# A row normalised in two halves, and its bias moved from VectorE to GpSimd, in a lattice attention kernel

## The chip, the cores and the metric

The kernel runs on one core of one Trainium2 chip. The metric is the device time in microseconds of one execution; the median of three runs is given. Engines: PE is TensorE, DVE VectorE, ACT ScalarE, POOL GpSimd, SP SyncE. Each takes its instructions in the order of the program and waits on semaphores for the others.

## The reference, cut to what matters

Eight sequences of 1024 tokens, 64 channels wide. An embedding comes first, then one "lattice" attention layer (8 heads of 64, so 8 x 8 = 64 pairs of sequence and head, called heads below), then a block of causal attention and a mixture of experts. The change is in the lattice layer:

```python
scores = einsum('bhqd,bhkd->bhqk', q, k) / sqrt(64)
int_scores = (abs(scores) * 1618).astype(int32)          # ttt_filter
chaos = int_scores % 9 in (0, 3, 6)
scores = scores * where(chaos, 1 / PHI, 1.0)
attn = softmax(scores, axis=-1)
attn = attn * (sin(C1 * attn) * exp(-attn**2 / PHI) + cos(C2 * attn))
ctx = einsum('bhqk,bhkd->bhqd', attn, v)
```

The softmax subtracts each row's maximum. The kernel gives it to the exponential as a bias, one number a row: bias = -EXPSCALE * maximum.

## The kernel before, in words

A head's scores are 1024 x 1024 fp32. They stand in `att` as eight tiles of 128 partitions (queries) by 1024 columns (keys); such a tile is called a row (of tiles) below, rows 0 to 7 of a head. `att` has two buffers, one for even, one for odd heads.

In `lattice`, the work on a head is cut into instructions that are placed on a time axis of steps by lists written out by hand. `SCORE` has the steps of the 16 score pieces (128 x 512, two to a row), `EXP` those of the 8 rows' exponentials, `GAUSS` and `SINE` those of the 8 transposed tiles on the way through exp(-x^2/PHI), sin and cos, `AV` those of the products with the values. A head stretches over three times `STEPS` = 88 steps; each pass `iteration(t, par)` walks through the 88 steps and issues what the lists put there for the heads t, t - 1 and t - 2. Every engine has a walk of its own through the same lists, and so a fixed order of its instructions; offsets such as `FILT` = 9 or `NORM` = 2 say how many steps behind the list's entry an instruction stands. A step is a place in that order, not a time: semaphores alone hold an engine up.

The instructions by name, with their lines:

- Score piece n of a head: PE product into one of three PSUM banks (L650); ACT absolute value (L502); POOL near op, to the nearest integer (L429, `RND` 2); DVE keep op (L561, `KEEP` 5); POOL factor op (L423, `FACT` 6); DVE filter op, which multiplies, writes `att` and keeps the row's maximum in `mx` (L570, `FILT` 9).
- Bias of row u: DVE, one column, `nb` = -EXPSCALE * `mx` (L578, `BIAS` 23 steps behind the row's second score piece).
- Row j: ACT exponential in place, with the row's sum (L466); DVE reciprocal of the sum (L537, `NORM` 2); POOL normalisation in place, times the reciprocal and times TURN (L418, `NORM` 2), 128 x 1024; DVE turn rounding of the row into `nturn`, bf16 (L549, `TURNS` 8), which waits for that row's normalisation.
- PE transposes (L608, `fill`), eight blocks of 128 x 128 for a pair of key blocks of four rows: tiles 0 to 3 wait until rows 0 to 3 are normalised, tiles 4 to 7 until all eight are. Each tile is transposed twice, once for the Gaussian part (ACT L495, L507, DVE L543, the ag product) and once for cosine and sine (ACT L478, DVE L520, PE L624, ACT L484, DVE L555).
- PE products with the values (L667), copied out by DVE (L526, L528); for each second head PE's fold (L674) and DVE's add to `hres` (L532).

The order on POOL by steps, around the change: near ops at 2, 5, 9, factor ops at 6, 9, 13, then the rows of the head before at 14, 16, 17, 19, 20, near ops at 23, 25, row 5 at 26, a factor op at 27, row 6 at 28, a factor op at 29, a near op at 30, row 7 at 34, and from there on factor and near ops alone. `held` is a wait with an empty instruction behind it on the sequencer. The semaphore `weights` counts the normalised rows, `filtered` DVE's filter ops, `bias` the biases.

Of the kernel before, what the change touches and what calls it, by code (L numbers as in the profile page):

```python
# [6 lines left out]
ALU = mybir.AluOpType  # L7
# [9 lines left out]
TB = S // P  # L17
# [8 lines left out]
EXPSCALE = 3.0 / (1618.0 * PHI * PHI)  # L26
TURN = C1 / (2.0 * math.pi)
# [3 lines left out]
def wait(eng, s, v):  # L31

    if not isinstance(v, int) or v > 0:
        eng.wait_ge(s, v)


def held(eng, s, v):

    if not isinstance(v, int) or v > 0:
        eng.wait_ge(s, v)  # L40
        eng.nop(nofuse=True)
# [226 lines left out]
def lattice(nc, ident, hres, xT_dram, wvo, Wq, bq, Wk, bk):  # L268

    RING = 4  # L270
    with ExitStack() as ctx:
# [15 lines left out]
        att = sb("att", [P, 2, TB, S])  # L287
# [5 lines left out]
        nb = sb("nb", [P, 2, TB])  # L293
# [102 lines left out]
        @block.gpsimd  # L396
        def _(pool):
            nc.gpsimd.memset(x[D:D + 1, :], 1.0).then_inc(consts, 1)
            pool.wait_ge(consts, 1)
            nc.gpsimd.memset(negI[:], 0.0).then_inc(consts, 1)  # L400
            pool.wait_ge(consts, 2)
            nc.gpsimd.affine_select(out=negI[:], in_=negI[:], compare_op=ALU.not_equal, fill=-1.0,
                                    base=0, pattern=[[-1, P]], channel_multiplier=1).then_inc(consts, 1)
            nc.gpsimd.memset(halfpi[:], math.pi / 2).then_inc(consts, 1)
            pool.wait_ge(consts, 4)
            nc.gpsimd.tensor_tensor(stack[:], ident[:, 0:D], ident[:, D:P], ALU.add).then_inc(consts, 1)
            pool.wait_ge(consts, 5)
            nc.gpsimd.memset(qT[:], 0.0).then_inc(consts, 1)
            pool.wait_ge(consts, 6)
            nc.gpsimd.memset(kT[:], 0.0).then_inc(consts, 1)  # L410

            def iteration(t, par):
                for s in range(STEPS):
                    for g, p, a in stages(t, par, s):
                        if a - NORM in EXP:
                            j = EXP.index(a - NORM)
                            held(pool, recip, TB * g + j + 1)
                            nc.gpsimd.tensor_scalar(att[:, p, j], att[:, p, j], rs[:, j:j + 1], TURN,  # L418
                                                    ALU.mult, ALU.mult).then_inc(weights, 1)
                        if a - FACT in SCORE:  # L420
                            n = SCORE.index(a - FACT)
                            held(pool, kept, NTILE * g + n + 1)
                            nc.gpsimd.tensor_scalar(mag[:, n % 4], mag[:, n % 4], 1.0, PHI,  # L423
                                                    ALU.mult, ALU.add).then_inc(factor, 1)
                        if a - RND in SCORE:
                            n = SCORE.index(a - RND)
                            held(pool, mags, NTILE * g + n + 1)
                            held(pool, kept, NTILE * g + n - 3)
                            nc.gpsimd.tensor_scalar(near[:, n % 4], mag[:, n % 4], 1.0 / 6.0, 1.0,  # L429
                                                    ALU.add, ALU.mult).then_inc(rounded, 1)  # L430

            over_heads(pool, iteration)
# [80 lines left out]
        def _(dve):  # L513
            def iteration(t, par):
                for s in range(STEPS):
# [22 lines left out]
                    for g, p, a in stages(t, par, s):  # L538
                        if a - AG in GAUSS:
                            d = GAUSS.index(a - AG)  # L540
                            wait(dve, gauss, TB * g + d + 1)
                            wait(dve, tmul, TB * (g - 1) + d + 1)
                            nc.vector.tensor_tensor(pair(ag[:, d]), turn_pair(d), pair(work[:, d % RING]),  # L543
                                                    ALU.mult).then_inc(agd, 1)
                        if a - TURNS in EXP:
                            j = EXP.index(a - TURNS)
                            wait(dve, nned, TB * g)
                            wait(dve, weights, TB * g + j + 1)
                            nc.vector.tensor_scalar(nturn[:, j], att[:, p, j], ROUND, -ROUND,  # L549
                                                    ALU.add, ALU.add).then_inc(turned, 1)  # L550
                        if a - P3 in SINE:
                            k = SINE.index(a - P3)
                            wait(dve, sined, TB * g + k + 1)
                            wait(dve, agd, TB * (g + 1))
                            nc.vector.tensor_tensor(sinb[:, k % RING], sinb[:, k % RING], ag[:, k],  # L555
                                                    ALU.mult).then_inc(tmul, 1)
                    for g, p, a in stages(t, par, s):
                        if a - KEEP in SCORE:
                            n = SCORE.index(a - KEEP)
                            wait(dve, rounded, NTILE * g + n + 1)  # L560
                            nc.vector.scalar_tensor_tensor(mag[:, n % 4], near[:, n % 4], 1.0, mag[:, n % 4],  # L561
                                                           ALU.mult, ALU.is_gt).then_inc(kept, 1)
                        if a - FILT in SCORE:
                            n = SCORE.index(a - FILT)
                            u, cols = n // 2, slice(n % 2 * 512, (n % 2 + 1) * 512)
                            wait(dve, factor, NTILE * g + n + 1)
                            wait(dve, filtered, NTILE * g + n)
                            wait(dve, xpose, NX * (g - 1))
                            dve.nop(nofuse=True)
                            nc.vector.tensor_tensor_reduce(  # L570
                                att[:, p, u, cols], mag[:, n % 4], score_bank(n), 1.0,
                                mx[:, p, n - 1:n] if n % 2 else -3.0e38, ALU.mult, ALU.max,
                                mx[:, p, n:n + 1]).then_inc(filtered, 1)
                        if a - BIAS in SCORE and SCORE.index(a - BIAS) % 2 == 1:
                            n = SCORE.index(a - BIAS)
                            u = n // 2
                            wait(dve, filtered, NTILE * g + n + 1)
                            nc.vector.tensor_scalar(nb[:, p, u:u + 1], mx[:, p, n:n + 1], -EXPSCALE, None,  # L578
                                                    ALU.mult).then_inc(bias, 1)

            over_heads(dve, iteration)

# [1 line left out]
        def _(pe):  # L584
# [16 lines left out]
            def fill(g, p, k):  # L601

                half = k // HALF
                wait(pe, weights, TB * g + TB // 2 * (half + 1))
                for c in range(2):
                    kt = 2 * k % TB + c
                    for i in range(4):
# [986 lines left out]
```

## Time and profile before

| | us |
|---|---|
| median of 3 runs | 5767.98 (5761.31 to 5770.59) |
| the profiled execution, its own time | 5762.87 |
| its span | 5761.0 |
| PE busy | 4760.1 (83%) |
| DVE busy | 4565.5 (79%) |
| ACT busy | 3985.3 (69%) |
| POOL busy | 2866.8 (50%) |
| lines of POOL in the lattice: factor op L423, near op L429, row L418 | 880.3, 779.2, 734.3 |
| bias of DVE, L578, x404 between 700 and 4200 us | 58.2 |

The span runs from the first to the last instruction. Busy times are sums over an engine's instructions; where they overlap waits of others they say nothing of what bounds the kernel. The first of the 64 heads' rows is normalised at 169 us, the last at 4554 us, and the lattice has the same pattern in between: heads about 69 us apart.

### The profile page before, as it was taken

The page shows a single profiled execution, that of the slowest core. Times are in us where ns is not written, and L with a number is a line of the kernel's source. Part 1 is how long each engine was busy: PE and PEld are TensorE (multiplying, and loading weights), DVE is VectorE, ACT ScalarE, POOL GpSimd, SP SyncE. Part 2 cuts the span into 40 slices and gives each one's busy share as a digit, 9 for nine tenths or more (in the row PEclk, how much of TensorE's full clock was granted, in tenths as well). Part 3 has the DMA queues.
Part 4 walks back from the last instruction along what each step waited for, and adds up shares of the span by engine and source line. Part 5 has one row for each costly group of instructions (what it writes and reads, how often), then busy time and mean ns, then how long its engine had stood idle before and what let it go on. Part 6 is the DMA issues. An engine that isn't in the chain of part 4 may idle for free. (4 is left out here: it accounts for less than half of the span.)

```text
span 5761.0 us, 97974 instructions
## 1 busy us (share of the span) xinstructions
PE 4760.1 (83%) x27689; PEld 2815.3 (49%) x27689; DVE 4565.5 (79%) x8035; ACT 3985.3 (69%) x5494; POOL 2866.8 (50%) x3215
## 2 busy tenths in 40 slices
PE   4788888888888888888888888888888769996999
PEld 2444444444444444444444444444444445554666
DVE  4788888888888888888888888888888656666664
ACT  2777787777877777787778778777777634443332
POOL 5555555555555555555555555555555334443233
PEclk9899999999999999999999999999999879998999
DMA  1000000000000000000000000000000000000000
GB/s 22 11 8 8 8 8 8 8 8 8 8 8 9 8 10 8 8 8 8 8 8 8 8 8 8 8 9 10 8 8 8 3 9 1 2 2 15 3 5 8
DMA packets 34197, 45.35 MB, mean 8 GB/s; under 512 B 24521, under 2 KB 24585, under 8 KB 34058
## 3 DMA queue, kind: packets, MB, share of 16 engines
q1 hardware_dynamic: 32010, 43.49, 2.8%
q0 software_dynamic: 2048, 0.14, 0.1%
q8 instruction: 72, 1.18, 0.1%
q14 instruction: 67, 0.55, 0.0%
HBM read 39.40 MB, written 4.19 MB: 8 GB/s over the span
## 5 line engine op out<-in xcount | busy, mean ns | idle before, releaser
L608 PE MATMUL banks<-ident,att 128*128 128x128 f32 x8192 | 1220.4, 300 | 533.4 <-DVE ag L543 339.2
L608 PEld LDWEIGHTS banks<-ident,att 128*128 128x128 f32 x8192 | 1027.9, 155 | 1094.0 <-DVE ag L543 539.6
L429 POOL TENSOR_SCALAR near<-mag 128x512 int32<-128x512 f32 x1024 | 779.2, 761 | 1257.0 <-ACT mag L502 1135.3
L650 PE MATMUL banks<-kT,qT 128*128 128x512 f32 x2048 | 1131.4, 642 | 60.3 <-DVE mx L570 59.0
L423 POOL TENSOR_SCALAR mag<-mag 128x512 f32<-128x512 f32 x1024 | 880.3, 864 | 567.9 <-DVE mag L561 532.5
L667 PE MATMUL outp<-work,vo 128*64 128x512 f32 x2048 | 960.6, 602 | 0.0
L667 PE MATMUL outp<-sinb,vo 128*64 128x512 f32 x2048 | 960.6, 602 | 0.0
L561 DVE SCALAR_TENSOR_TENSOR mag<-near,mag 128x512 f32<-128x512 int32 x1024 | 798.1, 784 | 110.1 <-POOL near L429 109.9
L478 ACT ACTIVATE work<-banks,halfpi 128x1024 f32<-128x1024 f32 x512 | 570.5, 1115 | 413.6 <-PE banks L608 311.5
L418 POOL TENSOR_SCALAR att<-att,rs 128x1024 f32<-128x1024 f32 x512 | 734.3, 1434 | 226.6 <-DVE rs L537 184.7
L520 DVE TENSOR_TENSOR work<-banks,work 128x1024 f32<-128x1024 f32 x512 | 624.7, 1220 | 158.2 <-ACT work L478 153.5
L495 ACT ACTIVATE work<-banks 128x1024 f32<-128x1024 f32 x512 | 521.1, 1021 | 301.1 <-PE banks L608 297.7
L555 DVE TENSOR_TENSOR sinb<-sinb,ag 128x1024 f32<-128x1024 f32 x512 | 673.7, 1316 | 2.1 <-ACT sinb L484 2.1
L543 DVE TENSOR_TENSOR ag<-banks,work 128x1024 f32<-128x1024 f32 x512 | 612.7, 1217 | 68.4 <-ACT work L507 62.2
L502 ACT ACTIVATE mag<-banks 128x512 f32<-128x512 f32 x1024 | 603.6, 590 | 47.0 <-PE banks L650 45.3
L484 ACT ACTIVATE sinb<-banks 128x1024 f32<-128x1024 f32 x512 | 523.7, 1023 | 115.6 <-PE banks L624 110.1
L466 ACT ACTIVATE att<-att,nb 128x1024 f32<-128x1024 f32 x512 | 582.2, 1138 | 0.8
L549 DVE TENSOR_SCALAR nturn<-att 128x1024 bf16<-128x1024 f32 x512 | 421.3, 833 | 145.8 <-POOL att L418 145.8
L507 ACT ACTIVATE work<-work 128x1024 f32<-128x1024 f32 x512 | 526.7, 1054 | 8.1
L667 PEld LDWEIGHTS outp<-work,vo 128*64 128x64 f32 x2048 | 248.9, 136 | 495.8 <-issue 481.1
L624 PEld LDWEIGHTS banks<-negI,nturn 128*128 128x128 bf16 x4096 | 260.9, 103 | 439.0 <-DVE work L520 357.1
L624 PE MATMUL banks<-negI,nturn 128*128 128x128 bf16 x4096 | 332.8, 227 | 134.5 <-DVE work L520 134.5
(197 smaller groups left out, 6387.9 us busy)
## 6 DMA issues: line engine op xcount, KB each, us to landing
x<-xT_dram SPq DMA_DIRECT2D x128, 256.0 KB, 3.5
xT_dram<-xT SPq DMA_DIRECT2D x8, 256.0 KB, 3.0
out<-hres SPq DMA_DIRECT2D x8, 256.0 KB, 2.6
base<-in_L_tok_turns,idx POOLq DMA_INDIRECT x64, 2.4
wqk<-in_L_attn_Wq SPq DMA_DIRECT2D x64, 16.0 KB
wqk<-in_L_attn_Wk SPq DMA_DIRECT2D x64, 16.0 KB
wqk<-in_L_attn_bq SPq DMA_DIRECT2D x64, 0.2 KB
wqk<-in_L_attn_bk SPq DMA_DIRECT2D x64, 0.2 KB
```

Of the source, the lines that this page charges most:

```text
L418: nc.gpsimd.tensor_scalar(att[:, p, j], att[:, p, j], rs[:, j:j + 1], TURN, ALU.mult, ALU.mult).then_inc(weights, 1)
L423: nc.gpsimd.tensor_scalar(mag[:, n % 4], mag[:, n % 4], 1.0, PHI, ALU.mult, ALU.add).then_inc(factor, 1)
L429: nc.gpsimd.tensor_scalar(near[:, n % 4], mag[:, n % 4], 1.0 / 6.0, 1.0, ALU.add, ALU.mult).then_inc(rounded, 1)
L502: nc.scalar.activation(mag[:, n % 4], score_bank(n), ACT.Abs).then_inc(mags, 1)
L520: nc.vector.tensor_tensor(pair(work[:, k % RING]), turn_pair(k), pair(work[:, k % RING]), ALU.mult).then_inc(acd, 1)
L543: nc.vector.tensor_tensor(pair(ag[:, d]), turn_pair(d), pair(work[:, d % RING]), ALU.mult).then_inc(agd, 1)
L555: nc.vector.tensor_tensor(sinb[:, k % RING], sinb[:, k % RING], ag[:, k], ALU.mult).then_inc(tmul, 1)
L561: nc.vector.scalar_tensor_tensor(mag[:, n % 4], near[:, n % 4], 1.0, mag[:, n % 4], ALU.mult, ALU.is_gt).then_inc(kept, 1)
L608: mm = nc.tensor.matmul(turn_pair(k)[:, c, i * P:(i + 1) * P], att[:, p, 4 * half + i, kt * P:(kt + 1) * P], ident[:], is_transpose=True, ...
L624: mm = nc.tensor.matmul(turn_pair(k)[:, c, i * P:(i + 1) * P], nturn[:, 4 * half + i, kt * P:(kt + 1) * P], negI[:], start=False, stop=Tru ...
L650: nc.tensor.matmul(score_bank(n), qT[:, p, (n // 2) * P:(n // 2 + 1) * P], kT[:, p, (n % 2) * 512:(n % 2 + 1) * 512], start=True, stop=Tru ...
L667: mm = nc.tensor.matmul(outp[rows], vo[:, kt, :], term[:, k % RING, c * 512:(c + 1) * 512], start=(kt == 0), stop=(kt == TB - 1), skip_gro ...
```

## The change

It does two things on the same steps. Each normalisation becomes two instructions of 512 columns, each of which adds one to `weights`; the waits for `weights` count twice as far, so that all who waited for a whole row, or four, still do. The bias is computed by POOL instead of DVE, at the same step (23 behind the row's second score piece); on POOL it is issued within a step ahead of the factor and near ops of the same head, and it waits for DVE's filter op through `held`. On DVE, bias and wait go. The instruction gets a second operation, + 0.0.

```diff
                             j = EXP.index(a - NORM)
                             held(pool, recip, TB * g + j + 1)
-                            nc.gpsimd.tensor_scalar(att[:, p, j], att[:, p, j], rs[:, j:j + 1], TURN,
-                                                    ALU.mult, ALU.mult).then_inc(weights, 1)
+                            for c in range(2):
+                                cols = slice(c * 512, (c + 1) * 512)
+                                nc.gpsimd.tensor_scalar(att[:, p, j, cols], att[:, p, j, cols], rs[:, j:j + 1], TURN,
+                                                        ALU.mult, ALU.mult).then_inc(weights, 1)
+                        if a - BIAS in SCORE and SCORE.index(a - BIAS) % 2 == 1:
+                            n = SCORE.index(a - BIAS)
+                            u = n // 2
+                            held(pool, filtered, NTILE * g + n + 1)
+                            nc.gpsimd.tensor_scalar(nb[:, p, u:u + 1], mx[:, p, n:n + 1], -EXPSCALE, 0.0,
+                                                    ALU.mult, ALU.add).then_inc(bias, 1)
                         if a - FACT in SCORE:
...
                             wait(dve, nned, TB * g)
-                            wait(dve, weights, TB * g + j + 1)
+                            wait(dve, weights, 2 * (TB * g + j + 1))
...
-                        if a - BIAS in SCORE and SCORE.index(a - BIAS) % 2 == 1:
-                            n = SCORE.index(a - BIAS)
-                            u = n // 2
-                            wait(dve, filtered, NTILE * g + n + 1)
-                            nc.vector.tensor_scalar(nb[:, p, u:u + 1], mx[:, p, n:n + 1], -EXPSCALE, None,
-                                                    ALU.mult).then_inc(bias, 1)
...
-                wait(pe, weights, TB * g + TB // 2 * (half + 1))
+                wait(pe, weights, 2 * TB * g + TB * (half + 1))
```

## Rows read from the trace of the kernel before

**Rows 1.** Busy time in one stretch, with the granted clock (PEclk, 1.00 is 2.4 GHz).
```profile
700.00:4200.00 3500.00, 2909.30 (x15956) 1656.81 (x15952) 3007.08 (x4970) 2769.24 (x3583) 1891.22 (x2015) 0.94 0.03 8
```

**Rows 2.** Groups, 700:4200: busy us, mean ns of one | idle before, who ended it.
```profile
L561 DVE SCALAR_TENSOR_TENSOR mag<-near,mag 128x512 f32<-128x512 int32 x806 | 628.9, 785 | 61.2 <-POOL near L429 61.2
L429 POOL TENSOR_SCALAR near<-mag 128x512 int32<-128x512 f32 x806 | 616.1, 764 | 992.6 <-ACT mag L502 895.6 <-DVE mag L561 71.5
...
L466 ACT ACTIVATE att<-att,nb 128x1024 f32<-128x1024 f32 x407 | 462.8, 1138 | 0.6
...
L549 DVE TENSOR_SCALAR nturn<-att 128x1024 bf16<-128x1024 f32 x402 | 330.0, 831 | 117.6 <-POOL att L418 117.6
```

**Rows 3.** Waits, 1000:4000: who, for whom: us in total, times, longest.
```profile
PE banks L608 <- POOL att L418: 132.6, 44, 3.0
```

**Rows 4.** Timeline of POOL, one head: start, us, what, count, idle before.
```profile
2113.20 0.62 POOL L429 TENSOR_SCALAR near<-mag 128x512 int32<-128x512 f32 x1
2114.70 0.62 POOL L423 TENSOR_SCALAR mag<-mag 128x512 f32<-128x512 f32 x1 [0.88 <-DVE mag L561]
2115.46 7.81 POOL L418 TENSOR_SCALAR att<-att,rs 128x1024 f32<-128x1024 f32 x5
...
2132.12 1.40 POOL L418 TENSOR_SCALAR att<-att,rs 128x1024 f32<-128x1024 f32 x1 [1.99 <-DVE rs L537]
```

**Rows 5.** Timeline of POOL, rows 0 to 3 of that head one by one.
```profile
2115.46 1.12 POOL L418 TENSOR_SCALAR att<-att,rs 128x1024 f32<-128x1024 f32 x1
2116.67 1.12 POOL L418 TENSOR_SCALAR att<-att,rs 128x1024 f32<-128x1024 f32 x1
2117.88 1.95 POOL L418 TENSOR_SCALAR att<-att,rs 128x1024 f32<-128x1024 f32 x1
2119.92 1.62 POOL L418 TENSOR_SCALAR att<-att,rs 128x1024 f32<-128x1024 f32 x1
```

**Rows 6.** Timeline of DVE, the same head.
```profile
2117.41 0.92 DVE L549 TENSOR_SCALAR nturn<-att 128x1024 bf16<-128x1024 f32 x1
...
2119.94 0.71 DVE L549 TENSOR_SCALAR nturn<-att 128x1024 bf16<-128x1024 f32 x1 [1.01 <-POOL att L418]
...
2125.44 0.14 DVE L578 TENSOR_SCALAR nb<-mx 128x1 f32<-128x1 f32 x1
2125.52 0.69 DVE L532 TENSOR_TENSOR hres<-outp,hres 128x512 f32 x1
```

**Rows 7.** Timeline of PE, the head before and this head.
```profile
2052.83 3.37 PE L608 MATMUL banks<-ident,att 128*128 128x128 f32 x16 [3.01 <-POOL att L418]
...
2121.60 1.97 PE L608 MATMUL banks<-ident,att 128*128 128x128 f32 x16 [3.01 <-POOL att L418]
```

**Rows 8.** POOL in the causal stage, 4600:5700: groups by width, then its timeline.
```profile
L862 POOL TENSOR_SCALAR c_pr<-c_pr,c_rs 128x1024 f32<-128x1024 f32 x32 | 35.8, 1119 | 50.8 <-DVE c_rs L1009 50.8
...
L862 POOL TENSOR_SCALAR c_pr<-c_pr,c_rs 128x512 f32<-128x512 f32 x32 | 22.1, 691 | 53.2 <-DVE c_rs L1009 53.2
...
L862 POOL TENSOR_SCALAR c_pr<-c_pr,c_rs 128x128 f32<-128x128 f32 x32 | 11.9, 372 | 38.7 <-DVE c_rs L1009 38.7
...
4718.22 0.91 POOL L862 TENSOR_SCALAR c_pr<-c_pr,c_rs 128x768 f32<-128x768 f32 x1 [2.74 <-DVE c_rs L1009]
4719.10 1.12 POOL L851 TENSOR_SCALAR c_qh<-c_q,c_own 128x1024 f32<-128x1024 f32 x1
```

**Rows 9.** Busy time around the two transposes of rows 7, with the granted clock.
```profile
2051.50:2056.00 4.50, 3.17 (x16) 3.17 (x17) 3.15 (x6) 1.27 (x3) 4.24 (x4) 0.62 0.00 0
2118.00:2124.00 6.00, 2.99 (x26) 2.40 (x23) 3.65 (x7) 3.79 (x7) 5.70 (x4) 1.00 0.00 0
```

**Rows 10.** Durations, ns min/median/max: near and keep ops, 700:4200; roundings, 1000:4000.
```profile
L429 POOL TENSOR_SCALAR near<-mag x806: 617/617/1556, 701.2 to 4193.7; 128x512 int32<-128x512 f32 x162
L561 DVE SCALAR_TENSOR_TENSOR mag<-near,mag x806: 670/687/1468, 703.6 to 4194.3; 128x512 f32<-128x512 int32 x162
...
L549 DVE TENSOR_SCALAR nturn<-att x349: 666/707/1148, 1004.3 to 3996.9; 128x1024 bf16<-128x1024 f32 x175
```

## The prediction

> **What bounds the kernel now.** I read the busy shares of a long steady stretch first, then who waits for whom, then the timeline of one head. No engine is full: DVE is busy 3007 of 3500 us (86%), PE 83%, ACT 79%, POOL 54% [rows 1]. So the order of the work across the four engines bounds it, and POOL, idle for nearly half of the time, can still be what the others wait for. It is: between 1000 and 4000 us PE waits for POOL's normalised rows 44 times, once a head (so a head takes some 69 us), 132.6 us together, 3.0 us a head [rows 3]. The timeline of one head says where. At 2115.46 POOL starts on the eight rows of a head; the first five run back to back, 7.81 us [rows 4]. Row 3, the fourth, ends at 2119.92 + 1.62 = 2121.54, and PE's transposes start at 2121.60, after 3.01 us with nothing to do [rows 5, 7]. I followed the waits back over 50 heads of the trace, from each instruction to the dependence, or the instruction before it on its engine, that ended last: this chain goes through rows 0 to 3 in every head, through row 4 in 21 of the 50, through one of rows 5 to 7 once: 4.4 rows a head. It comes to them along POOL: the factor op in front (2114.70, 0.62) ends 0.14 before row 0 starts [rows 4].
>
> One more thing is in these rows. An undisturbed row takes 1.12; row 2 takes 1.95 and row 3 1.62 [rows 5], since DVE's turn rounding (fp32 in, bf16 out) starts at the same moment and POOL stands still meanwhile. And the other way round: the rounding that starts at 2117.41, inside row 1, takes 0.92, the next 0.71 [rows 6]. A row and a rounding exclude each other.
>
> **The change, part by part.**
> (a) Each row in two halves. Another stage runs the same kind of POOL instruction, with a per-partition scalar, in eight widths: 1.119 at 1024 columns, 0.691 at 512, 0.372 at 128 [rows 8]. That is 0.83 ns a column and 0.26 us fixed. An undisturbed row of the lattice is 1.12 too, so a half is 0.691. The gap between two rows is 0.09 (2115.46 + 1.12 = 2116.58, the next starts at 2116.67) [rows 5]. So a row costs 2 x 0.691 + 0.09 - 1.12 = 0.35 us more. A rounding of DVE in between doesn't change that sum: it still waits for both halves, starts beside the first half of the next row, and holds that up as it now holds up the row. Nobody uses a half alone: the rounding of row j waits for 2(j + 1) halves, the transposes for all four rows of theirs. On the chain: 4.4 x 0.35 = 1.55 us a head. Rows 5 to 7 grow too, but they run between waits of POOL (row 7 at 2132.12 after 1.99 of idle time [rows 4]) and are on the chain in one head of 50: taken as nothing; were all eight rows on it, 8 x 0.35 = 2.8. The gap could be smaller: in another stage an instruction starts 0.03 before the one in front has ended (4718.22 + 0.91, then 4719.10) [rows 8], which makes 0.23 a row. I take 0.09, since it is the gap between these very instructions.
>
> (b) The bias leaves DVE. It shows 0.14 us, but the next instruction starts 0.08 after it (2125.44, 2125.52) [rows 6], so 0.07 to 0.08 of DVE's time; eight a head make 0.6. The chain as followed holds 1.6 of the eight: 1.6 x 0.07 = 0.11 us a head gained. Bounds: 0 and 0.6.
>
> (c) The bias comes to POOL, eight a head. No row shows a one-column tensor_scalar there. From below I take the fixed part of the near op, whose scalars are constants (0.617 at its fastest for 512 columns [rows 10], less 512 x 0.83 ns: 0.19), from above the 128-column instruction, 0.37 [rows 8]; value 0.2, with the gap 0.3. In POOL's order they stand at the steps 26, 44, 51, 60, 68, 74, 83 and 98, which is 10 of the next head. The one at 10 is the delicate one: it lies in front of the factor op of 2114.70, hence of all eight rows. But there POOL is idle for 0.88, waiting for DVE [rows 4]; without that cover it would be 0.3 a head. The one at 26 comes behind row 5, where the chain has left POOL; the other six stand where POOL waits for ACT or DVE (992.6 us of idle time before 806 near ops [rows 2]). Taken as nothing; bounds 0 and 8 x 0.3 = 2.4 a head. The new wait, for DVE's filter op, has always ended by then: ahead of each bias in POOL's order stands a factor op or a row whose own wait needs an instruction that DVE issues after that filter op. So nothing queues behind it. ACT's exponentials never waited for the bias (0.6 us idle before 407 of them [rows 2]) and the bias is ready many steps ahead of them on POOL as well.
>
> (d) TensorE's clock. PE's idle stretch before the transposes grows from 3.0 to 4.4 us. One head earlier the granted clock around this place is 0.62, here 1.00 [rows 9], and the same 16 transposes take 3.37 there and 1.97 here [rows 7]. A fall from 2.4 to 1.2 GHz so costs up to 1.4 us in a head. I take nothing, since the low level is there in many heads already; bounds -0.3 and +1.4 a head.
>
> Sum: 1.55 - 0.11 = 1.44 us a head, 64 heads: 92 us. The profiled execution took 5762.9 us (the span of 5761.0 and 1.9 around it), so it would take 5855; the median of the runs shown lies 5 above it: **5860 us**. All outside the lattice stays.
>
> **Rivals.**
> R1, faster: POOL gives the shared path back earlier and DVE gains more than POOL loses. DVE is the busiest engine and what needs that path is stretched: the 8 roundings of a head take 0.83 on the mean against 0.67 at best, the 16 keep ops 0.79 against 0.67 [rows 2, 10]: 8 x 0.16 + 16 x 0.12 = 3.2 us a head. If halves took half of it away and all eight biases counted, 1.6 + 0.6 = 2.2 against 1.55: 0.65 x 64 = 42 us faster, 5726. It decides from where more than 1.55 a head comes back on DVE. Against it: while the rows run DVE is idle for them (1.01 before the rounding at 2119.94 [rows 6]) and has no other use for the path; and much of the stretching is by the 512-column ops, which stay. The Trainium skill ("SBUF — State Buffer", section Who interferes with whom) speaks for this rival: VectorE and GpSimd share a pair of ports as a lock that the first to start holds for its whole instruction. The trace agrees (0.92 against 0.71 for the rounding [rows 6]).
> R2, slower by less: the second half starts without a gap. 4.4 x 0.23 - 0.11 = 0.9 a head, 58 us, 5826.
> R3, the longer idle stretch costs the clock in half of the heads: 1.44 + 0.7 = 2.1 a head, 137 us, 5905. For it: the same wait of 3.01 stands before the slow transposes and before the fast ones [rows 7], so the place is near the edge; against it, many heads are low already. The Trainium skill ("TensorE: Matmul & The Clock Gate", section What's actually happening) has an idle array fall to half its clock, which would favour R3.
> R4, no change: the longer rows fill slack and the bias pays for the rest, 5768. Against it stand PE's 3.01 us that end with row 3 [rows 7].
>
> **How the numbers follow.** Forecast 0.60 (its own range 5838 to 5890), R1 0.06, R2 0.16, R3 0.11, R4 0.07. A measurement of this kernel tells 0.2% (12 us) from no change. Faster 0.06, same 0.07, slower 0.87. The range leaves out R1, R4 and the far side of R3: 5800 to 5920.
>
> **What would show it.** Right: halves of 0.69 undisturbed, 0.09 apart; 7.5 us from the start of row 0 to the end of row 3, now 6.08; PE's wait for POOL's rows 4.4 us a head, as often as now; the bias on POOL 0.2 to 0.3 long, with no new wait behind it; POOL's busy time up by 64 x 8 x (0.26 + 0.2) = 236 us. Wrong: halves well under 0.69 or overlapping (R2); roundings and keep ops clearly shorter (R1); a granted clock in the steady stretch well under 0.94 [rows 1] (R3); a wait of POOL for the filter ops.

## The result, and the profile after

The changed kernel takes 5927.74 us (median of 6 runs, 5920.13 to 5930.42), the kernel before 5767.6 in the same series: ratio 1.0276, 95% interval 1.0265 to 1.0286, 160 us slower. That is 2.5 us for each of 64 heads, where 1.44 was forecast; the direction was right, and the time lies 8 us above the range. Where runs below are compared, both sides ran on one chip, and the ratio is the number to read, since the kernel before took from 5762 to 5788 us from chip to chip (medians).

The page of the kernel after. First busy time, then the DMA queue that carries instructions (packets, MB, share).

```profile
PE 4804.4 (81%) x27646; PEld 2841.5 (48%) x27689; DVE 4473.2 (75%) x7523; ACT 3987.2 (67%) x5494; POOL 3182.3 (54%) x4239
...
q14 instruction: 356, 2.91, 0.2%
```

POOL's busy time is 315.5 us up; 236 were expected from undisturbed durations. The other line was in no step of the prediction: q14 carried 67 packets before and carries 356 now, 8.2 KB each.

The stretch of [rows 1] and its groups, as in [rows 2].

```profile
700.00:4200.00 3500.00, 2837.39 (x15390) 1619.54 (x15389) 2827.16 (x4394) 2668.65 (x3447) 2056.06 (x2714) 0.93 0.03 8
```
```profile
L420 POOL TENSOR_SCALAR att<-att,rs 128x512 f32<-128x512 f32 x768 | 656.8, 855 | 147.5 <-DVE rs L545 80.2
L437 POOL TENSOR_SCALAR near<-mag 128x512 int32<-128x512 f32 x778 | 613.7, 789 | 800.5 <-ACT mag L510 734.5 <-DVE mag L569 39.6
L426 POOL TENSOR_SCALAR nb<-mx 128x1 f32<-128x1 f32 x390 | 110.8, 284 | 66.1 <-issue 36.9
...
L569 DVE SCALAR_TENSOR_TENSOR mag<-near,mag 128x512 f32<-128x512 int32 x778 | 582.1, 753 | 79.9 <-POOL near L437 79.9
L557 DVE TENSOR_SCALAR nturn<-att 128x1024 bf16<-128x1024 f32 x384 | 287.7, 755 | 164.7 <-POOL att L420 164.7
```

A near op now takes 789 ns on the mean (764), a keep op 753 (785), a rounding 755 (831). So DVE did get shorter operations, 16 x 0.032 + 8 x 0.076 = 1.1 us a head, as rival R1 had it, but it spends them waiting.

POOL's timeline of one head, to be read beside [rows 4, 5]: the burst, then its first half alone, its first two halves, and the seventh.

```profile
2115.97 0.70 POOL L426 TENSOR_SCALAR nb<-mx 128x1 f32<-128x1 f32 x1
2116.78 0.62 POOL L431 TENSOR_SCALAR mag<-mag 128x512 f32<-128x512 f32 x1
2117.53 9.71 POOL L420 TENSOR_SCALAR att<-att,rs 128x512 f32<-128x512 f32 x10
...
2117.53 0.69 POOL L420 TENSOR_SCALAR att<-att,rs 128x512 f32<-128x512 f32 x1
2117.53 1.48 POOL L420 TENSOR_SCALAR att<-att,rs 128x512 f32<-128x512 f32 x2
...
2123.21 1.19 POOL L420 TENSOR_SCALAR att<-att,rs 128x512 f32<-128x512 f32 x1
2131.80 0.19 POOL L426 TENSOR_SCALAR nb<-mx 128x1 f32<-128x1 f32 x1
```

A half takes 0.69 and two take 1.48, so the gap is 0.10. A half that meets a rounding takes 1.19 (DVE's rounding starts at 2123.15). Ten halves take 9.71, where five rows took 7.81. The bias takes 0.19 us in 414 of its 512 instructions and about 0.70 in 90, nearly all of which run beside DVE's keep op or its filter op with the running maximum; the longest takes 0.78.

PE's transposes of three heads (compare [rows 7]), the second of them in the head just shown, then the clock around the last pair.

```profile
2050.74 3.65 PE L610 MATMUL banks<-ident,att 128*128 128x128 f32 x16 [4.51 <-POOL att L420]
...
2125.24 1.97 PE L610 MATMUL banks<-ident,att 128*128 128x128 f32 x16 [2.09 <-POOL att L420]
...
2195.40 3.65 PE L610 MATMUL banks<-ident,att 128*128 128x128 f32 x16 [4.50 <-POOL att L420]
```
```profile
2195.00:2199.50 4.50, 4.10 (x20) 4.13 (x21) 2.15 (x4) 1.44 (x2) 4.15 (x5) 0.50 0.00 0
```

In the first and the last of them PE's wait is 4.5 instead of 3.0, and behind it the transposes run wholly at 1.2 GHz (granted clock 0.50). In the head of the burst above it is 2.1, and the transposes take 1.97. Over 50 heads (the ninth to the fifty-eighth) PE waits 4.5 us ahead of the first transposes in 25, and 1.8 to 3.6 in the others (mean of all 50: 3.6); before, it was 3.0 in all of them. They run wholly at the low clock in 33 of the 50, before in 14.

The waits, 1000 to 4000 us.

```profile
PE banks L610 <- POOL att L420: 182.6, 71, 4.5
DVE nturn L557 <- POOL att L420: 142.8, 142, 1.4
DVE sinb L563 <- issue: 46.9, 21, 2.4
POOL nb L426 <- issue: 32.4, 21, 1.7
```

PE's waits for POOL are 71 now and not 44 as before, 4.4 us a head together: there are short ones beside the long. The last two lines are new: 21 times, in every second head, DVE stands for 2.2 us at its first instruction behind the loop's jump without waiting for anything the profile shows, and POOL for 1.5 at its own. One of these stands, on DVE's timeline:

```profile
2252.76 1.55 DVE L563 TENSOR_TENSOR sinb<-sinb,ag 128x1024 f32<-128x1024 f32 x1 [2.17 <-issue]
```

### The profile page after: what moved, and what is told of

Same layout as the page of the kernel before. It is cut to its first block and busy times, and to the rows that moved or that the text cites. A ratio compares the mean times of both kernels' runs of the same rounds, so it can differ in the third digit from the quotient of the medians.

```text
span 5926.0 us, 99105 instructions
## 1 busy us (share of the span) xinstructions
PE 4804.4 (81%) x27646; PEld 2841.5 (48%) x27689; DVE 4473.2 (75%) x7523; ACT 3987.2 (67%) x5494; POOL 3182.3 (54%) x4239
## 5 line engine op out<-in xcount | busy, mean ns | idle before, releaser
L610 PE MATMUL banks<-ident,att 128*128 128x128 f32 x8192 | 1242.5, 304 | 591.6 <-DVE ag L551 306.8
L610 PEld LDWEIGHTS banks<-ident,att 128*128 128x128 f32 x8192 | 1050.2, 157 | 1151.4 <-DVE ag L551 535.8
L437 POOL TENSOR_SCALAR near<-mag 128x512 int32<-128x512 f32 x1024 | 801.4, 783 | 1060.2 <-ACT mag L510 972.8
L652 PE MATMUL banks<-kT,qT 128*128 128x512 f32 x2048 | 1146.6, 649 | 57.0 <-DVE mx L578 55.7
L420 POOL TENSOR_SCALAR att<-att,rs 128x512 f32<-128x512 f32 x1024 | 876.1, 856 | 204.9 <-DVE rs L545 115.2
L669 PE MATMUL outp<-work,vo 128*64 128x512 f32 x2048 | 973.1, 608 | 0.0
L669 PE MATMUL outp<-sinb,vo 128*64 128x512 f32 x2048 | 973.0, 609 | 0.0
L569 DVE SCALAR_TENSOR_TENSOR mag<-near,mag 128x512 f32<-128x512 int32 x1024 | 766.1, 753 | 140.4 <-POOL near L437 140.2
L557 DVE TENSOR_SCALAR nturn<-att 128x1024 bf16<-128x1024 f32 x512 | 385.2, 758 | 218.2 <-POOL att L420 218.1
```

What stands on the lines that cost most here:

```text
L420: nc.gpsimd.tensor_scalar(att[:, p, j, cols], att[:, p, j, cols], rs[:, j:j + 1], TURN, ALU.mult, ALU.mult).then_inc(weights, 1)
L610: mm = nc.tensor.matmul(turn_pair(k)[:, c, i * P:(i + 1) * P], att[:, p, 4 * half + i, kt * P:(kt + 1) * P], ident[:], is_transpose=True, ...
L652: nc.tensor.matmul(score_bank(n), qT[:, p, (n // 2) * P:(n // 2 + 1) * P], kT[:, p, (n % 2) * 512:(n % 2 + 1) * 512], start=True, stop=Tru ...
L669: mm = nc.tensor.matmul(outp[rows], vo[:, kt, :], term[:, k % RING, c * 512:(c + 1) * 512], start=(kt == 0), stop=(kt == TB - 1), skip_gro ...
```

## The experiments

Every number of this table is a mean over 50 heads (the ninth to the fifty-eighth) of the profiled run, in us, worked out from the trace: ends counted from the start of row 0, the first two groups of transposes together, the low-clock time of TensorE in two stretches of a head, and the distance between heads. Where rows are on DVE (e8, e12, e16) "row 3 ends" is the last of rows 0 to 3. A row of the table is one run: that of e7 is one of its four longer ones of ten (5754.02 us), those of e13 and e15 are their fastest (5710.67, 5696.41).

```
kernel                       row 3  2nd transp.  row 7  transposes  low clock  low clock  head
                             ends   ends         ends   1+2 take    0 to 22    34 to 50
before                       6.09    9.07        18.68  2.92         5.26       3.28      69.39
after                        7.51   10.76        21.59  3.15         6.80       2.66      72.10
e1  halves only              7.48   11.20        21.34  3.61         6.83       3.41      71.68
e2  bias only                5.74    8.33        18.75  2.44         5.32       3.62      70.57
e3  after, code aligned      7.49   11.20        21.44  3.61         6.69       3.48      71.68
e4  before, code shifted     5.56    8.30        18.50  2.45         4.71       2.46      70.09
e5  halves, PE kept busy     7.48    9.73        21.04  2.19         3.02       3.62      71.15
e6  before, PE kept busy     6.10    8.12        18.08  1.97         3.41       3.69      69.03
e7  rows 5-7 halved          6.09    8.93        19.55  2.78         6.35       2.73      69.49
e8  rows 1, 3 on DVE         3.26    5.36        16.59  1.96         5.12       3.41      68.27
e9  rows 0-4 halved          7.51   11.18        20.58  3.61         6.83       3.41      71.68
e10 the same, PE kept busy   7.48    9.70        19.94  2.16         3.28       3.41      70.56
e11 bias only, aligned       6.10    9.27        19.14  3.12         6.83       3.21      69.91
e12 row 3 on DVE             4.72    6.74        17.01  1.97         3.75       4.37      68.26
e13 after, rows 0-4 whole    6.09    9.57        19.51  3.42         5.53       0.14      68.45
e14 e7, PE kept busy         6.08    8.11        19.13  1.97         2.49       3.28      69.01
e15 score tile repeated      6.09    9.68        18.87  3.53         5.12       0.00      68.27
e16 e12 and e15              4.71    6.73        17.01  1.97         3.21       0.00      67.15
e17 e1 and e15               7.48   11.22        21.92  3.64        11.67       0.00      71.62
```

### The two parts alone, and the place of the code

**e1**: the halves and their counts of waits, the bias where it was.

> Only the rows in halves, bias on DVE as before. The halves' theory (each row 0.35 us longer, 4 to 5 rows a head on the chain) expects +1.5 to +1.8 us a head, +95 to +115 us, so 5863 to 5883. The rival, that code fetching makes the rest of the loss, says the same and adds that the loop's code is fetched no more than before (about 81 packets on the instruction queue q14, not 369). If the halves alone gave +150 or more, the fetches were no cause.

5928.45 us, ratio 1.0240 (1.0223 to 1.0257), 141 us over the kernel before on the same chip (5787.69). The halves alone cost 2.2 to 2.3 us a head, not 1.55, more than expected and with 68 packets on q14. (The expectations count every packet of the record, 81 and 369; the page those within the span, 67 and 356.)

**e2**: the bias on GpSimd, rows whole.

> Only the bias moved to POOL, rows whole. The halves' theory alone expects 0 to -7 us. The code fetch theory expects a stall of 2 us on DVE in each second head, as in the changed kernel, since DVE's loop body (349 instructions, shifted by 14) straddles one 128-instruction packet more: about +0.75 us a head, +40 to +50 us, with some five extra packets per pass of the loop (five, not ten: POOL's body, 282 long, still fits in three).

5847.04, ratio 1.0098 (1.0082 to 1.0115), with 210 packets on q14, 143 more than before. That is 59 us, more than either theory had.

**e3**: the full change with waits ahead of the loops that are satisfied long before, so that the loop bodies begin elsewhere in the code. An instruction has 64 bytes in the compiled program, a packet of q14 has 8192. In the kernel after, GpSimd's loop body (298 instructions) and VectorE's (349) each touch four such packets, in the kernel before (248 and 366) three.

```
+ for _ in range(12): held(dve, consts, 7)     # VectorE, ahead of its loop
+ for _ in range(50): held(pool, consts, 7)    # GpSimd
```

> The changed kernel with satisfied waits put ahead of the loop, 12 instructions on DVE and 50 on POOL, so that both loop bodies fit in three packets of 128 instructions. The fetch theory expects 45 to 55 us less than the changed kernel, 5873 to 5885, packets of q14 back to about 81. If fetches are harmless it is within 5 us of 5928.

5935.51, ratio 1.0254 (1.0237 to 1.0271), 66 packets; the stands at the loop's head are gone, but not the 45 to 55 us.

**e4**: the other way round. The kernel before, with VectorE's loop body moved to touch four packets.

```
+ for _ in range(50): held(dve, consts, 7)
```

> The kernel before with 50 instructions of satisfied waits ahead of DVE's loop, no other change, so that DVE's body straddles four packets. The fetch theory expects the stall of about 2 us on DVE once per two heads, half to three quarters of it on the chain: +30 to +55 us, 5798 to 5823. If fetches are harmless: 5768 to 5771 (50 short waits once, 3 us at most).

5833.5, ratio 1.0081 (1.0064 to 1.0098), with these lines in its page and its waits:

```profile
q14 instruction: 222, 1.82, 0.1%
```
```profile
DVE sinb L558 <- issue: 47.0, 21, 2.5
```

So a loop body over four packets instead of three is fetched again at each pass and costs 46 us here by itself. Undoing it in the full change gave back 0.2% only (1.0276 to 1.0254, and the two intervals overlap): with the stands the transposes took 3.15 us on the mean, without them 3.61, as in e1.

**e11**: e2 with the code in three packets each (14 waits ahead of VectorE's loop).

> Only the bias on GpSimd (ratio 1.0098 before), with 14 waits that are already satisfied put ahead of VectorE's loop, so that the loop bodies of VectorE and GpSimd lie in three packets of 8 KB of code each, as in the kernel before. Theory A, the 59 us were instruction fetches at the head of the loop: q14 goes from 210 packets to about 67 and the ratio to 0.999 to 1.003. Rival B, the bias itself or the added instructions on GpSimd cost it: the ratio stays above 1.007.

5786.87, ratio 1.0039 (1.0027 to 1.0052), 65 packets. Between the two: of the 1.0% of the bias 0.6 were the code's place, 0.4 (22 us) stay. In the table its second group of transposes ends 0.20 later and row 7 0.46 later, with more low clock in the first 22 us (6.83 for 5.26).

### Why the halves cost 2.3 and not 1.5

**e5** and **e6**: added matmuls that nobody reads, ahead of each head's wait for the first rows, four with the halves, three without.

```
+ if k == 0 and warm:
+     for _ in range(4):
+         nc.tensor.matmul(turn_pair(0)[:, 0, :], ident[0:D + 1, :], wvo[:], start=True, stop=True, ...)
  wait(pe, weights, ...)
```

> Halves only, with four more matmuls of 128x512 (fp32, of values that nobody reads, into the bank that the next transposes overwrite) put on TensorE ahead of each head's wait for the first four rows. Theory A, the clock is the second half of the split's price: TensorE stood idle for 4.45 us before those transposes in the split kernel and ran them at 1.2 GHz in all heads (3.62 us for the first two, low-clock share 0.97). With the added matmuls in that idle time the share falls under 0.4, the two transposes take about 2.5 us, and the time falls by 0.7 to 1.1 us a head, 45 to 70 us, to a ratio of 1.012 to 1.017 against the kernel before. Rival B, the halves cost 2.2 us a head on GpSimd alone and the clock follows without a price: the ratio stays at 1.022 to 1.026. Rival C, the added matmuls still run when the rows arrive: the ratio rises above 1.026.

> The kernel before with three such added matmuls. Theory A: its idle time there is 3.0 us and its low-clock share 0.64, so it has less to win: first two transposes from 2.94 to about 2.5 us, 0.3 to 0.5 us a head, ratio 0.992 to 0.997. Rival B (clock without a price): 1.000. Rival C (added matmuls in the way): 1.003 to 1.02.

e5: 5877.59, ratio 1.0189 (1.0172 to 1.0206). e6: 5740.77, ratio 0.9951 (0.9934 to 0.9967). The added matmuls (first line) and the transposes of one head of e5, and the clock around them:

```profile
2171.78 2.31 PE L608 MATMUL banks<-wvo,ident 65*128 65x512 f32 x5
2174.86 1.97 PE L614 MATMUL banks<-ident,att 128*128 128x128 f32 x16 [0.78 <-POOL att L420]
```
```profile
2174.00:2178.00 4.00, 3.23 (x30) 3.14 (x29) 1.53 (x4) 2.01 (x3) 3.65 (x5) 1.00 0.00 0
```

The clock did what it should, 1.97 for 3.65 (means 2.19 for 3.61). But e5 gained 0.5 us a head, not the 0.7 to 1.1 expected, and the distance between e5 and e6 is still 137 us, as e1's was 141. The clock was not simply the missing 0.7.

**e9** and **e10**: only rows 0 to 4 in halves, without and with the added matmuls.

```
- for c in range(2):
-     cols = slice(c * 512, (c + 1) * 512)
+ for c in range(2 if j < 5 else 1):
+     cols = slice(c * 512, (c + 1) * 512) if j < 5 else slice(0, S)
```

> The kernel before with rows 0 to 4 of each head in halves and rows 5 to 7 whole. The kernel with all rows in halves lost 2.2 us a head (ratio 1.0240), of which the later fourth row explains 1.40. Theory A, two paths side by side: TensorE starts its transposes 1.4 us later and loses 0.7 us more on them at 1.2 GHz, and GpSimd's own queue (rows 4 to 6, the roundings and factors between them) arrives as late by itself; either alone gives the whole 2.1. Shortening GpSimd's queue by three splits then changes nothing as long as the transposes run slow: ratio 1.021 to 1.025. Rival B, the price is spread over the rows: five eighths of it, ratio 1.014 to 1.016.

> The same with the four added matmuls that kept TensorE at 2.4 GHz. With all rows in halves they gave back only 0.5% (1.0240 to 1.0189), though the first two transposes ran in 2.18 instead of 3.62 us: by theory A because GpSimd's queue was then late by itself. Here that queue is three splits shorter, so now both paths are: the price over the kernel before with warm transposes (0.9951) is the later fourth row alone, 1.2 to 1.6 us a head, ratio 1.009 to 1.013. Rival B, the added matmuls give back 0.5% here too and no more: 1.016 to 1.020.

e9: 5901.58, ratio 1.0243 (1.0223 to 1.0263). e10: 5832.6, ratio 1.0121 (1.0102 to 1.0141). Both fell where the theory of two paths had them. In e9 rows 5 to 7 are whole and row 7 ends 0.76 earlier than in e1, and the time doesn't move, for PE's transposes end as late as in e1 (11.18). In e5 they end 1.5 earlier, and POOL's queue, row 7 at 21.04, is what comes last. Only with both out of the way, e10 against e6, does the price become that of the later fourth row: 70.56 - 69.03 = 1.53 us a head, or 1.70% by the ratios.

### Late rows, and a second place

**e7**: only rows 5 to 7 in halves (`j > 4` in the edit of e9).

> The kernel before with only rows 5 to 7 of each head normalised in halves, rows 0 to 4 whole. Theory A: the price of a half is paid on the rows that the first transposes and the first factors wait for; rows 5 to 7 are off the path, so three splits a head cost 0 to 0.15 us a head, ratio 0.999 to 1.002. Rival B: GpSimd's total time counts, 3 x 0.35 us a head, 67 us, ratio 1.011 to 1.013.

5715.41 (ten runs, 5693.35 to 5759.48), ratio 0.9918 (0.9894 to 0.9943). It costs nothing, as expected, but is faster and spread over 1.2%, with the run's granted clock between 0.927 and 0.953 in nearly the same order: four runs at 5742 us and more with 0.936 and less, six at 5716 and less with 0.946 and more.

**e14**: e7 with three added matmuls as in e6.

> Rows 5 to 7 in halves, with three added matmuls ahead of the first transposes. Without them the ten runs of this kernel lay between 5693 and 5759 us, the whole run's granted clock between 0.953 and 0.927 in the same order. Theory A, the spread is TensorE's clock in the transposes: with the added matmuls every run has them at 2.4 GHz, the spread falls under 0.3% as in the kernel before with added matmuls (5737 to 5746), and the ratio is 0.992 to 0.998. Rival B, the fast runs come from another stage: the spread stays near 1% and the fastest run near 0.987.

5733.56 (5729.5 to 5741.18), ratio 0.9951 (0.9937 to 0.9965): the spread is gone, and the ratio is e6's own. So three halved late rows cost nothing. That e7's spread is TensorE's clock fits the order of its runs, but theory A's place for it, the first transposes, isn't shown: with these at 2.4 GHz in every head of the profile, all of e14's runs (5729.5 and more) are longer than the six shorter ones of e7, none of which was profiled.

**e13**: the full change with rows 0 to 4 whole, the code in three packets.

> The full change with rows 0 to 4 whole again, rows 5 to 7 in halves, the bias on GpSimd, and satisfied waits ahead of the loops (14 on VectorE, 40 on GpSimd) so that both bodies lie in three 8 KB packets. Theory A, the halves of rows 0 to 4 are what the full change costs: what is left is the bias with its price of 1.0039 and GpSimd's queue, about 1.05 us longer over rows 5 to 7 with some 0.6 us of slack: ratio 1.002 to 1.010. Rival B, something of the full change that no single part showed: 1.015 or more.

5732.54 (5710.67 to 5754.9), ratio 0.9948 (0.992 to 0.9976), below what either theory had. The table, which has the fastest of the four runs, suggests a reason in its last columns: in the stretch from 34 to 50 us of a head TensorE has 0.14 us of low clock, where the kernel before has 3.28, although the first two groups of transposes got slower (3.42 for 2.92). In the other three runs the granted clock falls from 0.939 to 0.930 as the time grows. This is PE in two neighbouring heads of the kernel before, the slow one first:

```profile
2149.30 0.62 PE L624 MATMUL banks<-negI,nturn 128*128 128x128 bf16 x8 [0.85 <-DVE work L520]
2150.82 3.25 PE L686 MATMUL outp<-wvo,x 65*128 x16 [0.89 <-DMA x<-xT_dram]
...
2081.96 0.62 PE L624 MATMUL banks<-negI,nturn 128*128 128x128 bf16 x8 [0.85 <-DVE work L520]
2083.45 1.99 PE L686 MATMUL outp<-wvo,x 65*128 x16 [0.87 <-DMA x<-xT_dram]
```
```profile
2151.50:2160.00 8.50, 8.50 (x42) 6.64 (x44) 6.59 (x10) 4.13 (x6) 3.02 (x4) 0.61 0.13 35
2083.00:2089.00 6.00, 5.55 (x46) 4.58 (x48) 5.95 (x10) 4.88 (x8) 3.61 (x4) 1.00 0.19 49
```

The same instructions behind the same two gaps take 3.25 in one head and 1.99 in its neighbour. e15 tests whether the gaps are the cause.

**e15**: score tile 12 computed three times into the same bank, once and again at its place and once between the two gaps, with its signal on the last, so that both gaps are filled.

```
+ for _ in range(2 if n == 12 else 1):
      mm = nc.tensor.matmul(score_bank(n), ...)
+ if n != 12:
      mm.then_inc(qk, 1)
...
+ if a == SCORE[12] + 1:
+     nc.tensor.matmul(score_bank(12), qT[:, p, 6 * P:7 * P], kT[:, p, 0:512], ...).then_inc(qk, 1)
```

> The kernel before with one score product of each head (tile 12) computed three times over into the same bank instead of once, so that TensorE is busy in two gaps of 0.85 and 0.90 us about 34 to 37 us after a head's first row. Theory A: in the kernel before TensorE's clock falls to 1.2 GHz right behind these gaps in 30 of 50 heads (3.28 us of low clock a head between 34 and 50 us; in the full change with whole early rows 0.14 us a head, and its heads take 68.4 instead of 69.4 us). With the gaps filled that second place stays at 2.4 GHz: 3.28 / 2 = 1.6 us less of TensorE's time a head, of which some 1.0 to 1.5 us reach the period: ratio 0.983 to 0.990. Rival B, the fall there has another cause than the gaps: 0.998 to 1.004.

5708.89, ratio 0.9902 (0.9885 to 0.9919), at the edge of the expectation. The gain is net of a loss elsewhere, since the first two groups of transposes now take 3.53 for 2.92. No head has low clock in the second place any more:

```profile
2121.41 1.08 PE L630 MATMUL banks<-kT,qT 128*128 128x512 f32 x2
2122.40 1.99 PE L692 MATMUL outp<-wvo,x 65*128 x16
...
2122.00:2128.00 6.00, 6.00 (x48) 4.62 (x48) 6.00 (x10) 4.79 (x7) 3.61 (x4) 1.00 0.18 49
```

**e17**: the same with all rows in halves.

> All rows in halves (ratio 1.0240 alone; 2.3 us a head) and the repeated score product. Theory A: the price of the halves is paid in the first 15 us of a head and has nothing to do with the second place of low clock: this kernel gains as much as the kernel before does from the same edit and stands 2.1 to 2.4 us a head, 135 to 155 us, above it. Rival B: part of the 2.2 us was the second place, and the distance falls to about the 1.4 us of the later fourth row, 90 us.

5892.09, ratio 1.0215 (1.0195 to 1.0235). It gained 0.25% on e1, which the intervals don't tell from nothing, where the kernel before gained 1.0, and stands 183 us, 2.9 a head, above e15 (3.35 in the table, where e15 has its fastest run): neither theory had that. The low clock has left the second place and gone to the first, 11.67 us a head for 6.83. Two neighbouring heads, 13 us from 7 us behind the start of row 0:

```profile
2171.00:2184.00 13.00, 11.21 (x46) 9.66 (x47) 7.19 (x14) 6.10 (x8) 9.72 (x12) 0.50 0.00 0
2244.00:2257.00 13.00, 10.05 (x38) 7.32 (x39) 8.65 (x18) 8.40 (x10) 10.93 (x14) 0.65 0.00 0
```

In every second head TensorE stays at 1.2 GHz through the first three groups of transposes and most of the fourth, and these heads take 73.0 us; in the others the third group runs fast, and they take 70.2. So the price of the halves depends on what the clock does around them: 1.5 us a head for rows 0 to 4 with the transposes kept fast (e10, e6), 2.3 with nothing added (e9, and e1 for all rows), 2.9 for all rows in e15's surroundings.

### A better version

**e8**: rows 1 and 3 normalised by VectorE behind their reciprocal. **e12**: row 3 alone.

```
+ if j in ON_DVE:
+     wait(dve, recip, TB * g + j + 1)
+     nc.vector.tensor_scalar(att[:, p, j], att[:, p, j], rs[:, j:j + 1], TURN, ...).then_inc(weightsd, 1)
```

> The kernel before with rows 1 and 3 of each head normalised by VectorE right after their reciprocal, the other six by GpSimd. Theory A: TensorE and with it the whole loop wait for the fourth row; GpSimd's share of the first four rows falls from 6.1 to about 3 us and VectorE carries two operations of about 1 us each, on which it is late itself: -0.8 to -1.3 us a head, ratio 0.985 to 0.991. Rival B: VectorE is the engine that the rest of the chain runs on, and two more operations on it cost what they save: ratio 0.998 to 1.015.

> The kernel before with row 3 alone on VectorE (rows 1 and 3: ratio 0.9847, where the two operations delayed VectorE's first nturn by 0.9 us). Theory A: TensorE's first transposes start about 1.5 us earlier than before and VectorE pays for one operation: -0.9 to -1.4 us a head, ratio 0.981 to 0.988, at 2.4 GHz in most heads. Rival B: with three rows on GpSimd the fourth row still decides and it gains half of that: 0.990 to 0.995.

e8: 5682.94, ratio 0.9847 (0.983 to 0.9863), at the edge of theory A. e12: 5683.42, ratio 0.9862 (0.9843 to 0.9881), within it. The row takes 754 ns there, not 1120 and more:

```profile
L544 DVE TENSOR_SCALAR att<-att,rs 128x1024 f32<-128x1024 f32 x52 | 39.2, 754 | 1.8
```

**e16**: e12 with the repeated score tile.

> Row 3 on VectorE (ratio 0.9862 alone) and the repeated score product together. Its low clock in the second place was 4.37 us a head. Theory A: both gains add up, since one lies at the fourth row and the other 30 us later: another 1.3 to 1.9 us a head, ratio 0.960 to 0.970. Rival B: 0.983 to 0.988.

**5619.16 us, ratio 0.9746 (0.973 to 0.9763)**, less than theory A had (0.960 to 0.970) and more than B, since the gains themselves add up (1.4% and 1.0%). It is the fastest version here: 149 us faster than the kernel before, and 309 faster than the changed one by their medians. Its granted clock in the steady stretch is 0.98 ([rows 1]: 0.94).

```profile
700.00:4200.00 3500.00, 2972.51 (x16671) 1642.25 (x16672) 3164.33 (x5190) 2856.05 (x3704) 1939.90 (x2035) 0.98 0.03 8
```

## Why the prediction was right in direction and too small

**What bounds the kernel: right.** PE's wait ahead of the first transposes grew from 3.0 to 4.5 in every head of e1 and in half of those of the changed kernel, and the whole loop with it. (One reading was loose: row 2 of [rows 5] starts 0.47 behind the rounding of 2117.41, not with one. No term uses it.) e8 and e12, which take the burst of rows from POOL, gain 1.4 to 1.5%.

**(a) The halves: right on the burst, too small on the period.** 0.69 and a gap of 0.10; row 3 ends 7.51 behind the start of row 0 (7.5 expected, 6.09 before). e10 against e6 measures the term of rows 0 to 4 in the period: 1.53 a head for 1.55. "Taken as nothing" for rows 5 to 7 holds in e7, e9 and e14. It doesn't where the transposes are fast and the early rows late: e5 costs 0.7% (39 us) more than e10.

**(b) The bias off DVE** can't be told from the rest.

**(c) The bias on POOL, taken as nothing: low by a little.** 0.19 as expected where undisturbed, 0.284 on the mean, and with the code in place it costs 0.39%, 22 us, alone; beside the halves e3 against e1 leaves 0.14%. What of the 22 us is the instruction and what the clock (more of it low in e11) is not told apart.

**(d) TensorE's clock, "I take nothing": this is the step that failed.** The reason given, that it is low in many heads already, was half of the truth: before, 40 of 50 heads had some of it in the first two groups of transposes, but over only 0.63 of their time, and with the halves alone (e1) it is 0.97. There row 3 ends 1.39 us later, the second group 2.13 later, since the transposes take 3.61 for 2.92, and a head 2.3 more. The size of the term comes from rows 0 to 4 alone: their halves cost 1.70% with the clock kept (e10 against e6) and 2.43% without (e9), so the clock adds 0.73%, 42 us or 0.66 a head, where the sum had 0.

Rival R3 had this mechanism and the size (0.7 a head). What it did not have is that POOL's own queue was then as late as PE, so that removing the clock's part alone (e5) gave back a fifth of the price, no more than the same edit gives the kernel before (e6). The two terms taken as nothing, the clock in (d) and rows 5 to 7 in (a), lie on two paths side by side: each alone brings the same 0.7% (e9; e5 against e10), both together no more (e1).

In the changed kernel itself the transposes take only 3.15 on the mean, because the stands at the loop's head change where PE's wait falls in half of the heads; without the stands (e3) they take 3.61 too.

**What no step had: the code's place.** The longer body on POOL and the shifted one on DVE went from three packets to four, 67 packets to 356. In the bias alone it is 0.6% (e2, e11), in the full change 0.2% (e3).

The sum as measured, by the differences of the ratios of e1, e3 and the change: halves 2.40, bias beside them 0.14, code 0.22, together 2.76%. The bias beside the halves is small but clear on one chip (e1 5930.73 at most, e3 5933.59 at least), the code's place hardly. In us of 5768: 138 + 8 + 13 = 159.

**R1** was seen in its cause, not in its effect: DVE's operations are 1.1 us a head shorter. **R2** and **R4** fall by the gap of 0.10 and the 160 us. R3's rule in the Trainium skill ("TensorE: Matmul & The Clock Gate", section What's actually happening) agrees with the traces: 4.5 us without work, then 0.50 of the clock. Why it also falls behind the two gaps of under 1 us (e15) is not shown.

**Open**: why the low clock moves from the second place to the first in e17, and why it leaves the second in e13; why e7 takes less time in six of ten runs and the kernel before in none; what POOL's stand at the loop's head costs without DVE's (e2 and e4 have DVE's alone). A version of the full change with both places kept busy wasn't tried.

## What to carry to other kernels

A chain of waits gives the price of a longer operation only as long as the engine that waits runs at the same speed afterwards: where PE idles before its work, read the granted clock behind each such gap over many heads, and charge a longer gap with the slow version of what follows. Two paths that are late by the same amount hide each other: undo them singly and together, or each will look innocent. A place cured of the low clock can hand it to another, so look at the whole period afterwards. Before and after an edit of a loop, compare the packets of the instruction queue; a body that crosses one more packet can cost more than the edit.

## What the runs showed of the hardware

- Instructions come in packets of 8192 bytes. Loop bodies within three packets were not fetched again (65 to 68 packets in all), bodies over four were (210 to 356), at a stand of 2.2 us on the mean for DVE (e2, e4, the changed kernel) and 1.5 for POOL (the changed kernel) a pass. The Trainium skill ("Runtime: NRT & Kernel Launch", section Instruction fetch mechanics) gives most engines an instruction memory of 32 KiB, refilled in blocks of 16 KiB, has the crossing of a block mostly hidden and a jump back to a page that is no longer there as a stall. The stands right behind the loop's jump agree with the last, and e4 measures 46 us for them. By these sizes four packets of 8 KB would still fit if they filled two blocks, but VectorE's body begins 14 instructions earlier in e2 and 50 later in e4 than before, so that the fourth packet lies ahead of the three in one and behind them in the other, and both bodies are fetched again.
- TensorE's clock falls behind two gaps of 0.85 and 0.89 us (e15 fills them, and it no longer does) as well as behind one of 3.0, not in every head, and patterns repeat over two heads (e1: 72.9 and 70.5 us in turn).
- Filling a gap with matmuls whose result nobody needs gave 0.5% (e6, e5) and 1.0% (e15), but nothing clear of noise in e17, and e14 is slower than e7 (ratios 0.9951 and 0.9918).
- The same row takes 1120 ns on GpSimd undisturbed and 754 on the mean on VectorE (e12).
- A GpSimd instruction on one column takes 190 ns, or about 700 in 90 of 512 cases beside VectorE's work.
